# Expert blocks started before the last batch is routed, and two shared tiles moved to the end: one change to a transformer-layer kernel

## The reference: what is computed

```
x = x + attn(layernorm(x))                      # causal, one head of width 256, scores/16, softmax
xn = layernorm(x)
shared = (silu(xn Wg^T) * (xn Wu^T)) Wd^T       # inner width 512, every token
probs = sigmoid(xn router^T + bias)             # 8 experts, the best 2 per token, weights normed to sum 1
x = x + shared + sum over the 2 experts of weight * ((silu(xn gate_e) * (xn up_e)) down_e)
```

## Time and profile before

| | us |
|---|---|
| three timed runs | 561.99, 566.49, 566.75 |
| median | 566.49 |
| span of the profiled execution, first to last instruction | 555.3 |

### The profile page before, as it was taken

The page is one execution under the profiler, slowest core; times in us unless marked ns, Lnnn a source line. Parts: engine busy times, 40 slices in busy tenths (PEclk is TensorE's granted clock), DMA queues, the critical chain, the costliest instruction groups (busy, mean ns, idle before and its releaser), DMA issues.

```text
span 555.3 us, 14903 instructions
## 1 busy us (share of the span) xinstructions
PE 518.0 (93%) x4757; PEld 425.5 (77%) x4757; DVE 369.8 (67%) x980; ACT 301.0 (54%) x580; POOL 288.9 (52%) x242
## 2 busy tenths in 40 slices
PE   4889988999999999997999999999999999999992
PEld 3557766788878888886767788888787888888881
DVE  5788998689887878899747555445454454454551
ACT  3989877678777676744233443433343433434341
POOL 4466677668676765857022344452444434434443
PEclk9999999899999999998899999999999999999998
DMA  8799848949694947414465965764846536345443
GB/s 271 201 181 208 178 127 158 217 133 209 161 208 141 194 127 170 155 70 136 131 115 85 98 107 69 103 83 60 108 59 89 73 60 97 55 65 78 62 58 38
DMA packets 139351, 68.55 MB, mean 123 GB/s; under 512 B 114608, under 2 KB 132336, under 8 KB 139280
## 3 DMA queue, kind: packets, MB, share of 16 engines
q1 hardware_dynamic: 126128, 48.84, 43.5%
q0 software_dynamic: 13152, 18.76, 19.4%
HBM read 19.46 MB, written 23.08 MB: 77 GB/s over the span
## 4 chain that ended last, share of the span: by engine, by line
PE 65%; DVE 12%; DMA 8%; SPq 5%; ACT 5%; issue 3%; POOL 1%; POOLq 0%; ACTq 0%; DVEq 0%
PE bank L2216 29%; PE bank L2240 15%; PE bank L2547 4%; PE bank L2322 3%; PE bank L2564 3%; DMA v<-xnrow 2%; PE bank L2625 2%; PE bank L2347 2%; PE bank L2392 2%; DMA xn2t<-xrow 2%; PE bank L2369 2%; PE bank L2640 2%; SPq L405 2%; DMA x<-x 1%; DVE h L1470 1%
## 5 line engine op out<-in xcount | busy, mean ns | idle before, releaser
L2216 PE MATMUL bank<-xn2t,w 128*128 128x256 f16 x1608 | 184.9, 273 | 1.3 <-DVE th L1653 1.1
L2216 PEld LDWEIGHTS bank<-xn2t,w 128*128 (+1 forms) x1608 | 155.2, 98 | 24.3 <-DVE th L1653 2.2
L1644 DVE SCALAR_TENSOR_TENSOR th<-th,bank 128x512 f32<-128x512 f32 x83 | 56.6, 682 | 55.2 <-ACT th L989 54.1
L2240 PE MATMUL bank<-w,h 128*128 (+1 forms) x768 | 91.5, 273 | 0.0
L943 ACT ACTIVATE h<-th 128x512 f16<-128x512 f32 (+1 forms) x69 | 42.9, 622 | 84.6 <-DVE th L1653 78.3
L989 ACT ACTIVATE th<-bank 128x512 f32<-128x512 f32 x83 | 49.2, 593 | 62.1 <-PE bank L2216 47.6
L2240 PEld LDWEIGHTS bank<-w,h 128*128 128x128 f16 x768 | 74.0, 98 | 10.4 <-DVE x L1676 0.3
L866 POOL DMA_INDIRECT out<-p,wm x28 | 43.9, 1569 | 67.2 <-ACT p L1323 27.3
L1470 DVE TENSOR_TENSOR h<-th,h 128x512 f16<-128x512 f32 (+1 forms) x69 | 50.6, 733 | 38.3 <-ACT h L943 38.1
L734 POOL TENSOR_TENSOR w<-wst,w 128x768 f16<-128x768 f32 x36 | 59.1, 1645 | 18.9 <-ACT w L943 18.7
L758 POOL DMA_INDIRECT rows<-xrow,sidx x56 | 56.5, 1009 | 17.0 <-issue 13.3
(11 more groups left out here) (188 smaller groups left out, 808.4 us busy)
## 6 DMA issues: line engine op xcount, KB each, us to landing
wst<-w_all SPq DMA_DIRECT2D x36, 384.0 KB
x<-x SPq DMA_DIRECT2D x8, 512.0 KB, 5.6
out<-x SPq DMA_DIRECT2D x8, 512.0 KB, 4.0
rows<-xrow POOLq DMA_DIRECT2D x1, 1192.5 KB, 6.6
rows<-xrow,sidx POOLq DMA_INDIRECT x56
out<-p,wm POOLq DMA_INDIRECT x28
xn2t<-rows SPq DMA_TRANSPOSE x26
wm<-rows SPq DMA_DIRECT2D x26, 9.0 KB, 2.4
```

The lines of the kernel that those rows point to most:

```text
L1644: d.scalar_tensor_tensor(out=tb, in0=tb, scalar=1.0, in1=G[half][:, :], op0=ALU.add, op1=ALU.mult).then_inc(f_sg, 1)
L2216: ins = mm(dst, w_ap(j, ws, m * MAT + k * I + (2 * half + i) * P, P), moving(ms * KD + k), start=(cnt == 0), stop=(cnt == 3 * KD - 1))
L2240: ins = mm(o[:, a * D:(a + 1) * D], hb[:, (hs * KI + i) * TT + a * P:(hs * KI + i) * TT + (a + 1) * P], w_ap(j, ws, 2 * MAT + i * D, D), s ...
```

## The change

1. **Early blocks.** `SEEN` = 6: the count of the first 6 batches is taken by a new matmul (`counts_seen`). It gives `QUADS` = 5 blocks of 512 rows, of which three (pairs 0 to 5) are run first and two (pairs 22 to 25) last; 16 blocks of 256 rows lie between. Rows of a region are now filled from its start upward, with blank rows behind them (`zero_ends`, 8 DMAs of 128 rows in HBM) instead of blank rows in front written at the start for all 9 regions (`zero_rows`, 1192.5 KB, now one region). The first pairs wait only for the scatters of batches 0 to 5, all others for all scatters.
2. **Tables.** `table_of_quads` (18 steps) runs after `row_numbers(6)`, with its intermediate rows in PSUM; `table_of_pairs` (28 steps), `table_of_singles` and `table_of_halves` (30 together) run inside the new `plain_groups`. The scratch of the tables in SBUF moves to batch 2's part of x1.
3. **Order of the handover.** TensorE leaves the attention stage after tile 12 (`down(11)` moves in front of `shared_gate_up(13, 1)`, whole). `plain_groups` runs pairs 0 to 5 with nothing between but `down(13)`, batch 7's transposes, `logits(7)`, `prefix(7)` and `counts`. `scatter(7)` stands behind `y_add(0)` on GpSimd.
4. **Weights.** `w_low` is three instructions of 128x256, each waiting for the one before. On ScalarE `w_scale`/`w_high` of chunks 29 to 35 stand earlier, and on GpSimd `w_low(31)` to `w_low(35)` stand between single scatters of batch 6.
5. **End.** Shared tiles 14 and 15 run after the last expert block. SyncE waits until all adds have landed, reads their rows of `out` back to x1, VectorE adds the shared result, and plain DMAs write them. The quarter pieces of the last group are gone.

The core of the diff:

```diff
+SEEN = 6
+QUADS = -(-(SEEN * S * TOPK - E * (2 * TT - 1)) // (2 * TT))
+LAST = 2
+EARLY = 2 * (QUADS - LAST)
+PIECES = 3
+LATE = 2
+AHEAD = SHARED - LATE
+PLAIN = 3
...
                 pool.wait_ge(w_hi, g + 1)
-                cc.tensor_tensor(w_ap(j, 1, c * CH, CH), wst[:, (g % 2) * CH:(g % 2 + 1) * CH],
-                                 w_ap(j, 0, c * CH, CH), ALU.subtract).then_inc(w_lo, 1)
+                n = CH // PIECES
+                for i in range(PIECES):
+                    at = c * CH + i * n
+                    if i:
+                        pool.wait_ge(w_piece, g * (PIECES - 1) + i)
+                    cc.tensor_tensor(w_ap(j, 1, at, n), wst[:, (g % 2) * CH + i * n:(g % 2) * CH + (i + 1) * n],
+                                     w_ap(j, 0, at, n), ALU.subtract
+                                     ).then_inc(w_lo if i == PIECES - 1 else w_piece, 1)
...
             scatter(5, 1, 4)
+            table_iota()
             w_low(29)
             scatter(5, 4, 5)
             w_low(30)
             scatter(5, 5, 8)
             last_identity()
+            w_low(31)
+            w_low(32)
+            scatter(6, 0, 1)
+            w_low(33)
+            scatter(6, 1, 2)
+            w_low(34)
+            scatter(6, 2, 3)
+            w_low(35)
+            scatter(6, 3, 5)
             rstd2(7)
...
             w_scale(29)
+            w_high(29)
             tanh(11, 0)
             split_h(10, 1)
+            w_scale(30)
             logits_exp(6)
-            w_high(29)
-            w_scale(30)
+            w_high(30)
             tanh(11, 1)
             split_h(11, 0)
-            w_high(30)
+            w_scale(31)
+            w_high(31)
             split_h(11, 1)
-            w_scale(31)
+            w_scale(32)
+            w_high(32)
             tanh(12, 0)
-            w_high(31)
+            w_scale(33)
+            w_high(33)
             tanh(12, 1)
...
+            ffn_gate(12, 0)
+            ffn_up(12, 0)
+            ffn_gate(12, 1)
+            ffn_up(12, 1)
+            add_shared(10)
+            row_numbers(6)
+            table_of_quads()
+            ffn_low(12, 0)
+            ffn_gate(13, 0)
+            ffn_low(12, 1)
+            add_shared(11)
...
             shared_gate_up(13, 0)
-            last_transposes(0)
-            last_transposes(1)
+            shared_down(11, 0, 2)
             shared_gate_up(13, 1)
...
+            def plain_groups():
...
+                ffn(t + 2, 1)
+                ffn(t + 3, 0)
+                k = table_of_pairs()
+                ffn(t + 3, 1)
+                k = table_of_singles(k)
+                ffn(t + 4, 0)
+                table_of_halves(k)
+                ffn(t + 4, 1)
...
+            def last_group():
...
+                t = AHEAD + PAIRS
+                gate_up(t, 0, 0, half_batch(xn24(B - 1), 0), True)
+                pair_down(PAIRS - 1)
+                gate_up(t, 1, 0, half_batch(xn24(B - 1), 0), True)
+                gate_up(t + 1, 0, 0, half_batch(xn24(B - 1), 1), True)
+                gate_up(t + 1, 1, 0, half_batch(xn24(B - 1), 1), True)
+                down(t, 0)
+                last_down()
```

More of the change, by code:

```diff
@@ new lines, in zero_ends, with rows_complete @@
+            def zero_ends(first, last):
+                sp.wait_ge(tab2, 4)
+                for e in range(first, last):
+                    end = sp.value_load(end_tab[0:1, e:e + 1], min_val=0, max_val=ROWS - P)
+                    sp.dma_start(rows[ds(end, P), :], rows[SPARE:SPARE + P, :]).then_inc(pads_in, 16)
+            def rows_complete():
+                sp.wait_ge(rows_in[0], scattered(B - 2))
+                sp.wait_ge(rows_in[1], scattered(B - 1))
+                sp.wait_ge(pads_in, 16 * E)
@@ L2181, in _ @@
-            last_half()
+            last_group()
         @block.tensor
```

870 lines of the change are left out of this document (443 added, 427 removed).

## The result

| | before | after |
|---|---|---|
| median of 20 timed runs each, us | 563.72 | 569.41 |
| ratio after/before, 95% interval | | 1.0087 [1.0055, 1.0119] |
| profiled span, us | 555.3 | 564.1 |

The changed kernel is 0.9% slower, 4.9 us. The forecast was 0.1% faster. All ratios here leave out executions that are over 1.5% above the fastest of their kernel. In every run the device time is the profiled span plus 1.7 to 1.8 us. So the 7 to 11 us that the text ahead of the prediction put down to what lies before the first and after the last instruction, and the 11.2 us that the prediction added, were almost all difference between executions: the span of before (555.3) is shorter than that of any of its 20 timed runs (the fastest, 558.51, had some 556.8). The two spans therefore lie 8.8 us apart and the medians 5.7.

A forecast was written before the change was run, and what follows sets the result against it. TensorE was taken as the bound, so only its idle time and lower-clock losses counted. The terms -3.0 - 3.2 - 6.9 + 3.5 + 0.7 + 2.2 + 2.6 + 3.5 gave -0.6 us: 565.9 us, range 554 to 575.

The forecast's parts named there:

- the tables' paragraph: Plain groups: table steps make TensorE wait, 3.5 us lost; y copies not late by scatter 7 before y_add(1).
- another queue blocks the plain groups: Rival: pair rows wait on SyncE behind out_base(6), pair 2's land late and the clock falls; +6.0 us, 572.5, chance 0.08.
- early gain: Attention stage, 60 to 106 us: w_low in pieces holds VectorE for shorter times; 3.0 us gained, between 0 and 8.
- the end: Behind the last matmul: add, plain DMA and kernel end take 7.1 us against 10.3; 3.2 us gained, between 2 and 4.4.
- Handover: Attention to expert blocks: old gaps go, 6.9 us gained with the last group's 0.48; new waits of 3.5, 0.7 and 2.2 us.
- clock: Handover: matmuls at 1.2 GHz behind the new gaps; 2.6 us lost, between 0 and 5.4.
- (c): Handover, before the first pair: chunk 35's w_low ends at 246.5, TensorE is there at 244; 2.2 us idle, between 0 and 4.5.
- (a): Handover: tanh(12, 1) behind w_scale(33) on ScalarE delays add_shared(10), for which down(11) waits; 3.5 us idle, between 0.5 and 4.1.
- the weights keep up: Rival, handover: faster loads or a less late ScalarE leave smaller waits and no clock loss; -8.4 us, 558.1, chance 0.33.
- end of the kernel, 3.6 us: Tail: time left from the last add's landing at 551.7 to 555.3, taken over unchanged from the kernel before.
- Tables in the plain groups: Plain groups: table steps on VectorE make ffn(17, 1) 1.2 us late, ffn(18, 0) 2.1; 3.5 us lost, between 1 and 6.
- The rival in which they lose it: w_low's pieces lose the port to VectorE between pieces, a chunk costs 1.4 us more; +6.6 us, 573.1, chance 0.16.

The follow-up runs named there:

- e8: The changed kernel with a fixed expert 0 for the matmuls of pairs 3 and 4; ratio 1.0084 to the kernel before.
- e6: The changed kernel with the table of pairs moved behind VectorE's work on the second chunk; ratio 1.0165 to the kernel before.
- e5: The changed kernel with GpSimd starting batch 7's eight scatters only after the table of pairs; ratio 1.0325 to the kernel before.
- e7: The changed kernel with batch 7's eight scatters in four pairs, one y_add behind each; ratio 0.9983 to the kernel before.
- e13: The changed kernel as it is, run a third time; ratio 1.0143 to the kernel before.
- e14: The kernel of e7 (changed kernel, batch 7's scatters in four pairs) run again, beside e13; ratio 1.0002 to the kernel before.
- e18: e14 with the table of pairs in two parts, singles and halves a chunk later, tanh(12, 1) ahead of chunk 33's scale; ratio 0.9853 to the kernel before.
- e3: The kernel before with only w_low cut into three pieces; ratio 1.0030 to the kernel before.
- e1: The changed kernel run again, with no edit; ratio 1.0056 to the kernel before.
- e2: The changed kernel with w_low whole again, one 128x768 piece per chunk; ratio 1.0099 to the kernel before.
- e11: The changed kernel with fixed expert 0 for pairs 3 and 4 and pair 5's rows loaded ahead of pair 4's aux; ratio 1.0009 to the kernel before.
- e15: The kernel of e8 (changed kernel, fixed expert 0 for pairs 3 and 4) run again, beside e13; ratio 1.0201 to the kernel before.
- e16: The changed kernel with the table of pairs behind the second chunk and pair 5's rows ahead of pair 4's aux; ratio 1.0233 to the kernel before.
- e9: The changed kernel with y_add(1) ahead of batch 7's eight scatters on GpSimd; ratio 1.0091 to the kernel before.
- second set: The runs e5 to e8, edits of the changed kernel sharing one chip with runs of the kernel before; ratios 1.0325, 1.0165, 0.9983 and 1.0084.

## Why the prediction was wrong, point by point

**The step that failed** is the last but one sentence of the tables' paragraph: "Scatter 7 (8 x 1.27 us) stands before `y_add(1)`; the y copies have four buffers and are not late by it." It priced the delay of `y_add(1)` by the y buffers alone, at nothing. The duration was right (10.2 us from the first scatter to the add), the consumer was missed: SyncE's aux load of pair 4 waits for that add, and the rows of pair 5 are listed behind it. That was to be read from the code and from SyncE's list. What the runs show in its place is a wait of 5.27 us for these rows, with 1.6 us of clock behind it (e8; 8.41 and 15.36 us in e6 and e5, where the scatters start later), and 5.6 us gained where spreading takes it away with no crawl in either profile (e7 beside e8). The rival "another queue blocks the plain groups" names the mechanism with another place (pair 2, behind `out_base(6)`), at +6.0 us and a chance of 0.08.

**What no step had** is the crawl. It costs 8.7 us in the profile after, and it lies over the late rows, so that the two are paid once. With the rows late and no crawl (e8) the ratio is 1.0084, in the range of the changed kernel's three. The crawl alone was in no run. Both go when the scatters are spread, 7.9 us (e13, e14). Then the changed kernel stands at 1.0002 and 0.9983, near the forecast's -0.1%. That is in part luck: the early gain of 3.0 us can't be found, and the end gave 2.4 us more than forecast.

**What held.**
- Handover: 2.90 + 0.36 + 2.74 for 3.5 + 0.7 + 2.2, clock 3.1 for 2.6. In (c) `w_low(35)` ended at 247.4 for 246.5, and the reading of the expert's number (1.5 us) was not in the sum; TensorE came to it at 246.2 for 244, which hid that. The prediction had (c)'s start hang on `row_numbers(6)`, and so on (a). What it did not draw from it is that one call in front of chunk 33 moves both: 5 us (e18). The rival "the weights keep up" did not come: loads land 3.1 us from issue, and ScalarE still waits for them.
- The end: 4.7 us behind the last matmul for 7.1. The term "end of the kernel, 3.6 us" was too large: from the issue of the last DMA (561.21, 0.96 us for two) to the last instruction are 2.9 us, its landing included. The forecast had 6.4 us for landing and end together. Gain 5.6 for 3.2.
- Tables in the plain groups: 3.5 us forecast, 1.78 + 0.36 + 2.11 = 4.25 measured without a crawl (e14); in the changed kernel one of 1.43 us is left (at 307.7), the others lie under the crawl.

**What was too high.** The early gain of 3.0 us does not show in the milestone of tile 13, nor in the number of matmuls done by 106 us (722 for 721). The gaps did shrink: 2.24 us is 0.62 and the clock loss of 1.6 us behind it is gone, 46.00 - 40.70 = 5.3 us idle for 6.4. But the fill of the first 20 us holds 1.6 us less matmul work (8.79 for 10.42, a clock of 0.93 for 1.00). It does so in e3 too, which is built from the kernel before, and less in e1, the changed kernel again (10.12): part of it is a difference between executions. New gaps of 0.53 and 0.76 us at the routing of batches 5 and 6 took more. In the kernel before the pieces gave nothing (e3).

**The pieces and the port.** The rival in which they lose it is refuted. A piece took 687 ns, four of the 108 took 1.0 us or more, and three with their waits took 2.17 to 2.53 us at the handover. No VectorE product with two SBUF inputs there took over 0.80 us, where one took 4.12 us before. The rule of the Trainium skill ("SBUF — State Buffer", two separate sides) is that who comes first keeps the port pair for the whole instruction; so a held operation should wait as long as the one GpSimd instruction in front of it, and the trace agrees. The longest such VectorE operation after, 1.71 us at 94.84, stood beside a GpSimd operation of 2.13 us that the change does not cut (L793, 93.86).

**What stays open** is the cause of the crawl. Shown: of 13 profiles with batch 7's eight scatters in one run beside pairs, 10 have it; of 5 with the scatters in twos none has, two of these on chips where it was there beside them. On TensorE it starts 6 to 8 us after the first scatter and ends within 1 us of the last indirect add of the run. TensorE's semaphore counts raised just ahead of it are seen late, mostly by about 8 us, and ScalarE, which waits for one of them, stands still before TensorE slows (from 283.3 us in the profile after). VectorE's small steps come 0.7 us apart in it, while GpSimd keeps its 1.27 us a scatter. Not needed for it are the pieces (e2), TensorE's register instructions (e11, e15), a table beside it (e16) and scatters that start ahead of `y_add(1)` (e9). Three profiles escaped it with the same run of scatters. All three are of the second set's chip, on which the changed kernel was not run, and e8's kernel crawled on another chip (e15): whether it is the chip or the loading of the program, no experiment tells. One rival was not tested. The traces hold DMA loads of instructions, 8 KB each. The one that comes 12.1 to 12.5 us behind its predecessor in the eight profiles without a crawl that are made from the changed kernel comes 14.9 to 22.9 us behind in nine of the ten with one. In the changed kernel it was due at 284.1 us, after ScalarE had stopped, and in e9 it came in time and the crawl was there all the same, so it may be a consequence. Whether the profiler's own records play a part can't be told either, since every execution here was profiled.

## What to carry to other kernels

When a long job is put ahead of a short one in a queue, follow the short one's completion to every entry that waits for it, and then read what is listed behind those entries in their own queues; free buffers are only one consumer. When a gap disappears and the time stays, look for a second limit of the same length under it, and take both away at once before calling either harmless. Two waits in one handover, one behind the other, can hang on one cause: move the earliest and see whether the later one moves with it. One execution's profile can lie several us from another of the same lists, so compare stages only beside runs of the same chip.

## What the runs showed of the hardware that was not expected

- Beside eight indirect scatters from GpSimd in one run (0.96 us each, 0.30 between) the other engines were slow in 10 of 13 profiles: TensorE one matmul per 0.7 us or more instead of 0.11, increments by its matmuls seen after some 8 us instead of 0.29. In twos between indirect adds they were not in 5 of 5, though in e7 and e14 ten and in e18 fourteen such calls followed one another at most 0.5 us apart.
- The length of one gap does not say whether TensorE falls to 1.2 GHz behind it. Twenty-four matmuls took 4.24 and 4.46 us behind gaps of 2.90 and 2.74 (granted clock 0.65 and 0.62), but 2.79 behind 2.86 (1.00) and 4.45 behind 2.23 (0.63) in e14, and 2.85 behind 2.69 (1.00) in e18.
- Reading one expert's number into TensorE stands between the end of its wait and the next matmul: 1.5 us in the changed kernel and in e18 (wait over at 247.42 and 243.15, matmul at 248.96 and 244.66).
